# One slot for a batch's value matmuls, maxima split on GpSimd, and another order of the prologue, in a fused attention and feed-forward block

## What is computed

```python
x = x + tanh(g_xattn) * xattn(layernorm(x), ctx, ctx)     # per head: q, k, v are 8 x 256
    # qk = einsum('dq,dl->ql', q, k) / sqrt(8); sm = softmax(qk); out = einsum('ql,dl->dq', sm, v)
x = x + tanh(g_ffn) * ffn(layernorm(x))
    # a = quant8(x) @ ternary(w_gate).T ; b = quant8(x) @ ternary(w_up).T      (256 -> 1024)
    # h = silu(a) * b ; h = rms_norm(h, ln_weight) ; quant8(h) @ ternary(w_down).T (1024 -> 256)
```

## Time and profile before

| | us |
|---|---|
| median of 3 runs | 220.3 |
| lowest, highest | 218.5, 220.82 |
| the profiled execution | 220.69 |
| its span, first to last instruction | 218.9 |

### The profile page before, as it was taken

One profiled execution on the slowest core, in us unless ns is written; L12 is line 12 of the kernel. 1 busy time (PEld: TensorE's weight loads), 2 busy tenths in 40 slices (PEclk: granted clock), 3 DMA queues, 4 the chain that ended last, 5 costly groups with the idle time before them and its releaser, 6 DMA issues. The chain is left out here.

```text
span 218.9 us, 3965 instructions
## 1 busy us (share of the span) xinstructions
PE 155.9 (71%) x1307; PEld 79.6 (36%) x1314; DVE 168.5 (77%) x343; ACT 133.4 (61%) x265; POOL 110.4 (50%) x195
## 2 busy tenths in 40 slices
PE   0023886839895898979898998999988972463343
PEld 0021442424452534434355553645533441230221
DVE  6818999725775767489896988889849979899981
ACT  3400426816899896948678586869879872163330
POOL 5824868835600598598838875758741103111010
PEclk9999999976999999999999999999999999589555
DMA  3496799899692644272163156121021100000001
GB/s 96 133 206 183 217 352 369 227 307 314 158 270 53 160 130 125 57 214 78 31 171 93 40 132 163 30 76 32 27 76 34 46 28 0 9 15 24 0 0 48
DMA packets 21955, 25.85 MB, mean 118 GB/s; under 512 B 4374, under 2 KB 18966, under 8 KB 20918
## 3 DMA queue, kind: packets, MB, share of 16 engines
q1 hardware_dynamic: 20040, 21.36, 35.2%
q10 hardware_dynamic: 1896, 4.26, 5.9%
HBM read 18.20 MB, written 7.19 MB: 116 GB/s over the span
## 5 line engine op out<-in xcount | busy, mean ns | idle before, releaser
L935 DVE TENSOR_REDUCE mx<-sr 128x2 f32<-128x512 f32 x128 | 82.1, 679 | 16.9 <-PE sr L1212 16.6
L718 ACT ACTIVATE pr<-sr 128x512 f32<-128x512 f32 x128 | 71.4, 601 | 13.3 <-PE sr L1234 12.9
L1212 PE MATMUL sr<-ks,qs 128*128 128x256 bf16 x256 | 51.5, 298 | 24.0 <-DMA ks<-scr_k 19.4
L1234 PE MATMUL sr<-qs,ks 128*128 128x256 bf16 x256 | 49.1, 278 | 5.8 <-DVE kh L1022 2.9
L1247 PE MATMUL ob<-pr,vw 128*32 128x256 f32 x512 | 41.1, 394 | 3.5 <-ACT pr L718 2.1
L1212 PEld LDWEIGHTS sr<-ks,qs 128*128 128x128 bf16 x256 | 21.3, 104 | 52.7 <-issue 25.1
L1234 PEld LDWEIGHTS sr<-qs,ks 128*128 128x128 bf16 x256 | 22.1, 99 | 18.0 <-DVE kh L1022 3.8
L1287 PE MATMUL sr<-wt,xt 128*128 128x512 bf16 x57 | 16.1, 407 | 3.2 <-ACT xt L758 2.0
L1321 PE MATMUL sr<-wt,ht 128*128 128x256 bf16 x64 | 10.7, 316 | 9.0 <-ACT ht L816 5.3
L1247 PEld LDWEIGHTS ob<-pr,vw 128*32 128x32 f32 x512 | 10.3, 108 | 18.0 <-ACT pr L718 9.7
L768 ACT ACTIVATE kh<-sr,ghs 128x512 f32<-128x512 f32 x16 | 10.9, 687 | 7.6 <-PE sr L1287 7.5
(11 more groups left out here) (123 smaller groups left out, 249.9 us busy)
## 6 DMA issues: line engine op xcount, KB each, us to landing
qs<-scr_q SPq DMA_DIRECT2D x7, 576.0 KB
ks<-scr_k SPq DMA_DIRECT2D x21, 192.0 KB
scr_o<-osb SPq DMA_DIRECT2D x14, 128.0 KB, 3.8
scr_k<-kp SPq DMA_DIRECT2D x8, 192.0 KB, 5.3
scr_q<-qp SPq DMA_DIRECT2D x8, 192.0 KB, 5.4
scr_k<-kp SPq DMA_DIRECT2D x8, 128.0 KB, 5.5
wf<-in_wg ACTq DMA_DIRECT2D x1, 1024.0 KB, 7.1
wf<-in_wu ACTq DMA_DIRECT2D x1, 1024.0 KB, 10.3
```

Source lines behind the costliest of these rows:

```text
L718: nc.scalar.activation(pr[:, b % PR_BUFS, m % 4, :], bank("score", m)[:, :], ACT.Exp, scale=float(DH) ** -0.5).then_inc(exp_done, 1)
L935: nc.vector.tensor_reduce(mx[:, h % 2, first + 2 * at:first + 2 * at + 2], bank("max", n)[:, :].rearrange("p (c n) -> p c n", c=KC), axis= ...
L1212: mm = nc.tensor.matmul(bank("max", n)[:, c * COLS:(c + 1) * COLS], qs[:, t % STACKS, at:at + P], ks[:, t % STACKS, u * COLS:(u + 1) * COL ...
L1234: mm = nc.tensor.matmul(bank("score", m)[:, c * COLS:(c + 1) * COLS], ks[:, t % STACKS, at:at + P], qs[:, t % STACKS, u * COLS:(u + 1) * C ...
```

## The change

- A batch's value matmuls, c = 0 and c = 1, run in one slot, VALUES = 6 after the batch's first score.
- POOL splits a group's maxima in slot hi into a bf16 part and the remainder (split_maxima). PE transposes both with one bf16 transposition in slot hi + 4, ACT casts them into the rows that SP writes in hi + 5. cut_maxima, its padding and constants go away.
- Prologue: pair 0 of x and context and the three gates are loaded right after tiles 0 and 1; the mean of pair 0 comes before the second and third memset of qs. split_pair becomes five parts with slots of their own; so do first_parts and second_parts on ACT.
- LATE, LATE_NORM = 6, 7: tiles 4 and 5 are weighed and scaled on POOL, tiles 5 and 6 get attention and norm there. Slots in AT and the other tables are changed. The weights are loaded in slots 5, 18, 24.

```diff
--- before.py
+++ after.py
@@ -28,16 +28,15 @@
 VBUFS = 3
 
 LAG = 20
+VALUES = 6
 PR_BUFS = 3
-LATE, LATE_NORM = 4, 5
+LATE, LATE_NORM = 6, 7
 BANKS = 7
 TURNED = TILES - 1
-CAST = 3
-CUT = 3
-SHIFT = 4
-TURN = 3
-PAD = 16
-SMALL = PAD + 2 * 8 + PAD + 2 * 4
+CAST = 4
+SPLIT = 0
+SHIFT = 5
+TURN = 4
...
-    "copy1": [37, 55, 72, 86, 104, 119, 133, 150],
-    "invert": [48, 64, 79, 94, 112, 124, 138, None],
-    "inv_out": [44, 61, 82, 95, 108, 124, 140, None],
-    "inv_in": [47, 61, 82, 98, 118, 124, 147, None],
-    "attention": [53, 68, 83, 97, 115, 128, 149, 155],
-    "norm": [58, 73, 90, 104, 124, 133, 150, 166],
-    "scale_x": [62, 76, 92, 110, 124, None, None, None],
-    "weigh": [80, 86, 106, 117, None, None, None, None],
-    "scale_y": [80, 94, 110, 127, 140, 165, 176, 189],
-    "down": [97, 109, 128, 139, 156, 172, 187, 199],
-    "result": [98, 110, 127, 137, 164, 168, 194, 208],
+    "copy1": [38, 55, 70, 85, 102, 118, 133, 151],
+    "invert": [54, 60, 78, 95, 110, 126, 138, None],
+    "inv_out": [48, 61, 82, 94, 106, 126, 150, None],
+    "inv_in": [53, 62, 82, 94, 113, 128, 151, None],
+    "attention": [58, 69, 86, 101, 114, 131, 146, 157],
+    "norm": [65, 73, 92, 105, 123, 131, 149, 166],
+    "scale_x": [68, 75, 93, 111, 123, 138, 154, None],
+    "weigh": [84, 89, 107, 118, 139, 153, None, None],
+    "scale_y": [86, 97, 112, 127, 139, 165, 176, 192],
+    "down": [101, 111, 130, 138, 157, 185, 199, 211],
+    "result": [101, 111, 129, 136, 165, 181, 207, 231],
...
-PAIR_AT = [0, 18, 30]
-LOAD_AT = [0, 2, 10]
-VALUES_AT = 16
-WEIGHT_AT = [12, 27, 33]
-ABS_AT = [43, 48, 51]
-ROUND_AT = [53, 57, 69]
-CUT_AT = [57, 58, 71]
-NORM_W_AT = 65
+MEAN_AT = [17, 18]
+NORM_AT = [0, 18, 26]
+CUT_K_AT = [0, 17, 40]
+CUT_Q_AT = [0, 21, 36]
+LAST_K_AT = [1, 32, 47]
+LAST_Q_AT = [2, 35, 51]
+FIRST_K_AT = [0, 16, 31]
+FIRST_Q_AT = [0, 25, 33]
+NEXT_K_AT = [6, 19, 44]
+NEXT_Q_AT = [1, 31, 36]
+PARTS_AT = [1, 30, 42]
+LOAD_AT = [0, 2, 5]
+GATES_AT = 0
+VALUES_AT = 19
+WEIGHT_AT = [5, 18, 24]
+ABS_AT = [46, 49, 50]
+ROUND_AT = [54, 58, 68]
+CUT_AT = [52, 61, 77]
+NORM_W_AT = 64
 SUM_W_AT = 52
-STACK_AT = 4
-FILL_AT = [4, 13, 20]
-CONST_AT = 31
+STACK_AT = [23, 41, 48, 66, 84, 97]
+FILL_AT = [7, 16, 21]
+CONST_AT = 3
...
-        mx = sb("mx", [P, 2, SMALL + 2 * 4 + 2 * 4], F32)
-        mh = sb("mh", [2 * 2 * 8, 2, P], BF16)
+        mx = sb("mx", [P, 2, 2 * 8], F32)
+        mxp = sb("mxp", [P, 2, 2, 2 * 8], BF16)
...
@@ -390,6 +399,9 @@
 
             load_xk(0, 1, 0)
             load_xk(1, 2, 1)
+            load_pair(0)
+            for n, g in enumerate((gx_d, gf_d, gamma_d)):
+                sp.dma_start(gates[:, n:n + 1], g.rearrange("(a n) -> a n", a=1).to_broadcast((P, 1))).then_inc(gate_in, DMA)
             sp.wait_ge(k2_cast, 1)
             sp.wait_ge(k3_done, 1)
             k_to_dram(0)
@@ -399,7 +411,6 @@
             sp.wait_ge(k_out[0], 2 * DMA)
             sp.wait_ge(k_ones, 1)
             load_keys(0, 0, HALF, early_in)
-            load_pair(0)
             sp.wait_ge(k2_cast, 2)
             sp.wait_ge(k3_done, 2)
             k_to_dram(1)
@@ -407,8 +418,6 @@
             sp.wait_ge(q3_done, 2)
             q_to_dram(1)
             load_keys(0, HALF, SPAN, stack_in[0])
-            for n, g in enumerate((gx_d, gf_d, gamma_d)):
-                sp.dma_start(gates[:, n:n + 1], g.rearrange("(a n) -> a n", a=1).to_broadcast((P, 1))).then_inc(gate_in, DMA)
             next_stack(1)
             load_values(0, 0, 2)
 
@@ -418,12 +427,12 @@
                 for pair in range(PAIRS):
                     if pair >= 1 and n == LOAD_AT[pair]:
                         load_pair(pair)
-                    if n == PAIR_AT[pair] + 12:
+                    if n == PARTS_AT[pair]:
                         parts_to_dram(pair)
                 if n == VALUES_AT:
                     load_values(1, 2, TILES)
-                if n % PER == STACK_AT and 2 <= n // PER + 1 < TILES:
-                    next_stack(n // PER + 1)
+                if n in STACK_AT:
+                    next_stack(2 + STACK_AT.index(n))
                 for r in range(2):
                     t = due(f"sums{r}", n)
                     if t is not None and t < TURNED:
...
+            def norm_pair(pair):
 
                 two = slice(2 + 2 * pair, 4 + 2 * pair)
-                q = qf[:, two, :].rearrange("p t n -> p (t n)")
-                k = kh[:, two, :].rearrange("p t n -> p (t n)")
                 rstd_q(two.start, two.stop)
                 step(nc.gpsimd.tensor_scalar(nm[:, two], mv[:, two, 0], -1.0, None, ALU.mult))
                 pool.wait_ge(q_rstd, two.stop)
                 for t in range(two.start, two.stop):
                     nc.gpsimd.tensor_scalar(qf[:, t, :], xh[:, t, :], nm[:, t:t + 1], rs[:, t:t + 1],
                                             ALU.add, ALU.mult).then_inc(q_normed, 1)
+
+            def cut_keys(pair):
+
+                k = pair_of(kh, pair)
                 pool.wait_ge(k1_cast, 3 + pair)
                 nc.gpsimd.tensor_tensor(k, k, high_half(k), ALU.subtract).then_inc(k1_left, 1)
+
+            def cut_queries(pair):
+
+                q = pair_of(qf, pair)
                 pool.wait_ge(q1_cast, 3 + pair)
-                pool.wait_ge(q_normed, two.stop)
+                pool.wait_ge(q_normed, 4 + 2 * pair)
                 nc.gpsimd.tensor_tensor(q, q, high_half(q), ALU.subtract).then_inc(q1_left, 1)
+
...
+            def split_maxima(h):
+
+                rows = group_rows(h)
+                pool.wait_ge(max_taken, GROUPS[h][1])
+                if h >= 2:
+                    pool.wait_ge(max_turned, h - 1)
+                parts = mxp[:, h % 2, :, :].rearrange("p n r -> p (n r)")
+                high = high_half(mx[:, h % 2, :])[:, 0:rows]
+                nc.gpsimd.tensor_copy(parts[:, 0:rows], high).then_inc(max_split, 1)
+                nc.gpsimd.tensor_tensor(parts[:, rows:2 * rows], mx[:, h % 2, 0:rows], high, ALU.subtract).then_inc(max_split, 1)
 
...
+                if n - SPLIT in ENDS:
+                    split_maxima(ENDS[n - SPLIT])
                 if n in FILL_AT:
                     first_values(FILL_AT.index(n))
-                for pair in range(1, PAIRS):
-                    if n == PAIR_AT[pair]:
-                        split_pair(pair)
+                for pair in range(PAIRS):
+                    if n == NORM_AT[pair]:
+                        norm_pair(pair)
+                    if n == CUT_K_AT[pair]:
+                        cut_keys(pair)
+                    if n == CUT_Q_AT[pair]:
+                        cut_queries(pair)
+                    if n == LAST_K_AT[pair]:
+                        last_keys(pair)
+                    if n == LAST_Q_AT[pair]:
+                        last_queries(pair)
                 if n == CONST_AT:
                     late_constants()
                 if p == 0 and VBUFS <= T < TILES:
-                    pool.wait_ge(pv_done, 8 * (T - VBUFS + 1))
+                    pool.wait_ge(pv_done, 4 * (T - VBUFS + 1))
                     fill_values(T)
...
                                      scale=float(DH) ** -0.5).then_inc(exp_done, 1)
@@ -723,12 +752,12 @@
                 rows = 2 * group_rows(h)
                 act.wait_ge(max_turned, h + 1)
                 if h >= 2:
-                    act.wait_ge(max_cut, h - 1)
-                nc.scalar.activation(mh[0:rows, h % 2, :], bank("turn", h)[0:rows, 0:P], ACT.Copy).then_inc(max_cast, 1)
+                    act.wait_ge(shift_in[h % 2], shifts_in(h - 2))
+                nc.scalar.activation(mp[0:rows, h % 2, :], halves_of("turn", h)[0:rows, 0, :], ACT.Copy).then_inc(max_cast, 1)
...
                 if 0 <= n - LAG < TOTAL:
                     exp(n - LAG)
                 for pair in range(PAIRS):
-                    if n == PAIR_AT[pair] + 4:
-                        first_parts(pair)
-                    if n == PAIR_AT[pair] + 8:
-                        second_parts(pair)
+                    if n == FIRST_K_AT[pair]:
+                        act.wait_ge(k_in[2 + pair], DMA)
+                        key_pair(pair, 0, k1_cast)
+                    if n == FIRST_Q_AT[pair]:
+                        act.wait_ge(q_normed, 4 + 2 * pair)
+                        query_pair(pair, 0, q1_cast)
+                    if n == NEXT_K_AT[pair]:
+                        act.wait_ge(k1_left, 3 + pair)
+                        key_pair(pair, 1, k2_cast)
+                    if n == NEXT_Q_AT[pair]:
+                        act.wait_ge(q1_left, 3 + pair)
+                        query_pair(pair, 1, q2_cast)
+                if n == GATES_AT:
+                    act.wait_ge(gate_in, 3 * DMA)
+                    nc.scalar.activation(tg[:, :], gates[:, 0:2], ACT.Tanh).then_inc(tanhed, 1)
                 if n in WEIGHT_AT:
...
+            def mean_pair(pair):
+                dve.wait_ge(x_in[2 + pair], DMA)
+                for t in (2 + 2 * pair, 3 + 2 * pair):
```

(50 more changed lines are left out.)

100 lines of the change are left out of this document (40 added, 60 removed), and 18 rows, old and new, of the table AT.

## The result

| | before | after |
|---|---|---|
| median, us | 219.87 | 223.36 |
| lowest to highest | 218.5 to 220.82 | 222.37 to 224.1 |
| span of the profiled execution | 218.9 | 220.9 |
| mean granted clock | 0.933 | 0.883 |

The changed kernel is slower: ratio 1.0136, 95% interval 1.0084 to 1.0189, where 206 us was forecast. The stretch from maximum 64 to 127 and the tail became a little shorter; the loss stands before maximum 32, where the largest single gain was expected.

What follows compares the result with a forecast made beforehand. PE was taken to set the pace in slots 64 to 128, DMA share 0.90 the early stretch, DVE the tail. Gains of 5 + 2.5 + 3 + 1 + 3 = 14.5 us gave a 204.4 span, said as 206 us; range 199 to 216.

Steps and rivals of the forecast that it cites:

- The prologue's first maximum: Prologue: first maximum starts at 15.4 instead of 20.27 us, 4.9 earlier, with PE's first matmul at 14.8.
- The weights are also loaded earlier … I take 5 us by maximum 32: Up to maximum 32: 5 us gained despite earlier weight loads in a stretch of DMA share 0.90; bounds 2 and 8.
- The prediction's own sign of being wrong: Wrong if the first maximum starts early but maximum 32 does not, or POOL's splits start over four slots late.
- rival (2): Early stretch: DMA eats the early gain, stack 2 lands near 47 as before; 9.5 gained, 211 us; chance 0.10.
- The split behind the first fill: Early stretch: POOL's first fill, waiting for a values load, precedes group 1's split; could eat some of the 5 us.
- Rival (4): Slots 56 to 144: split behind late POOL work, PE waits at each transposition; slower, 227 us; chance 0.08.
- Values in one slot: Value matmuls: sixteen records together in 1.00 us save PE 0.25 a batch, 32 batches; bounds 0.11 and 0.36.
- The transposition: Transposing maxima: one bf16 transposition for a float32 one saves PE 0.60 us a group, 18 groups.
- Slots 64 to 128: Middle: PE paces and gives back 8.8 us, POOL's load grows to 62; stretch 71, 3 us gained; bounds 0 and 8.8.
- Slots 32 to 64: PE gives back 4.4 of 34.8 us, 1.9 off for SP's waiting writes and shift; 2.5 gained; bounds 0 and 5.
- 128 to the last value matmul: Slots 128 to 148: ACT busy 19.23 of 22.1 us, its work unchanged; 1 us gained; bounds 0 and 2.
- Tail: After the last value matmul: DVE sheds 5.6 of 31.76 us, POOL's chain grows; 3 us gained; bounds -2 and 6.

Runs made afterwards that it cites:

- e5: Kernel before with only the prologue's new order (pair 0, gates, mean of pair 0), weights at old slots: 217.75 us, ratio 0.9892 to before.
- e4: Kernel before with only a batch's value matmuls put in one slot: 220.16 us, ratio 1.0001 to before.
- e20: Kernel before with only the two more tiles on GpSimd and the new AT slots for tiles 4 to 7: 220.31 us, ratio 1.0073 to before.
- e16: e5 with the weights loaded at slots 5, 18, 24 instead of 12, 27, 33: 222.4 us, ratio 1.0096 to before.
- e11: Changed kernel with the weights loaded at the old slots 12, 27, 33: 219.03 us, ratio 1.0027 to before.
- e1: Changed kernel with POOL's first fill of values in slot 9 instead of 7: 222.71 us, ratio 1.0096 to before.
- e2: Changed kernel with the split of maxima on DVE instead of POOL, same slot: 220.33 us, ratio 0.9947 to before.
- e13: e9 with transposition 3 and shift 4 slots after the group, split on POOL: 243.63 us, ratio 1.115 to before.
- e12: e10 with transposition 3 and shift 4 slots after the group, split on DVE: 217.0 us, ratio 0.9939 to before.
- e19: e12 with the two more tiles on GpSimd and the new AT slots for tiles 4 to 7: 217.25 us, ratio 0.9795 to before.
- e3: Changed kernel with e1 and e2 together (later first fill, split on DVE): 218.62 us, ratio 0.9894 to before.
- e14: Changed kernel with e11, e1 and e2 together (old weight slots, later fill, split on DVE): 218.51 us, ratio 1.001 to before.
- e9: Changed kernel's forms with all slots of the kernel before, tiles 4 to 6 in DVE's form, split on POOL: 238.04 us, ratio 1.0769 to before.
- e10: e9 with the split of maxima on DVE instead of POOL: 230.23 us, ratio 1.0428 to before.
- e7: Changed kernel with tiles 4 to 6 back in DVE's form: 225.09 us, ratio 1.0208 to before.

## Why the prediction was wrong

**The prologue's first maximum** was right in kind and mis-sized: 16.94 instead of 15.4. I held PE's first matmul at 14.8; it went to 16.3. The first write went out at 5.23, 0.1 later, so the five issues cost nothing on SP, as said; but the loads of pair 0 and the gates are now issued ahead of that write, and SP, which waits for the write to land, issues the first keys at 9.40, for 7.68 before. The term of 4.9 measured 3.3, and in e5 2.8; against the 19.2 to 19.4 that two executions with the old prologue show (e4, e20) it is about 2.

**"The weights are also loaded earlier … I take 5 us by maximum 32"** is the step that failed: 5 us of gain forecast, 4.1 of loss measured. It named the DMA share of 0.90 and the moved loads, and then priced them at nothing. In this stretch a load moved ahead of a stack delays it: 1 MB is 3.8 us by rate and 4.65 as measured in e16, and with the weights back at their slots maximum 32 of the changed kernel comes 5.1 earlier (e11). The prediction's own sign of being wrong came true: the first maximum is early and maximum 32 is not. My bounds of 2 and 8 held no loss at all, though rival (2) had said that the early gain could be eaten; it took "stack 2 lands near 47 as before" as the worst, and stack 2 let PE go on at 51.60. The issue slots in the diff were enough to price it.

**The split behind the first fill** was seen too ("now stands ahead of the split of group 1. Of these any can eat some") and priced at nothing for the same 5 us. The wait was 9.24. Alone it is worth little (e1: 0.65), since the keys stand 4.98 behind it; with the rest on DVE it is 3.0 (e2).

**Rival (4)** had 0.08 and the wrong place. That its 227 us is the nearest figure to 223.4 is luck. Its mechanism is real and up to 26.6 us big (e13), but in the changed kernel PE's waits for the split between maxima 64 and 127 come to 1.6 us (the three longest of PE there; then DVE's longest):

```profile
PE sr L1298 <- ACT xi L780: 3.2, 1, 3.2
PE sr L1257 <- DVE mx L972: 2.1, 1, 2.1
PE sr L1247 <- POOL mxp L573: 1.6, 2, 0.9
```

```profile
DVE am L1005 <- POOL xn L592: 7.4, 4, 3.1
```

The waits for xn and xi, 3.7 and 0.8 us in the kernel before, look like work that is late because it stands behind the split on POOL. The split is not their main cause: with it on DVE at the same slots (e2), PE waits 3.4 us for xi there and DVE 5.0 for xn. Which of the other new slots makes them longer was not measured. The groups of after, busy and mean ns as in the earlier trace rows, with the idle time before:

```profile
L572 POOL COPY mxp<-mx 128x16 bf16<-128x16 bf16 (+1 forms) x18 | 3.5, 195 | 14.1 <-DVE mx L972 14.1
L573 POOL TENSOR_TENSOR mxp<-mx 128x16 bf16<-128x16 f32 (+1 forms) x18 | 3.8, 212 | 0.0
L625 POOL TENSOR_TENSOR wf<-wf,lnw 128x1024 f32<-128x1024 f32 x6 | 14.2, 2360 | 2.4 <-DVE wf L1059 2.4
```

The split itself costs 0.41 a group against 0.5 forecast. The copy of 16 columns took 197 ns and that of 8 columns 190, so nearly all of it does not depend on the width.

**Values in one slot**: right in size by starts, 16 records in 1.00 (112.08 to 113.08; by busy time e4 gives back 2.8 of the 4.0 counted from maximum 64 on), and wrong in what it is worth: e4 gives nothing.

**The transposition** saves 0.40, not 0.60: its record takes 0.16 and 0.09 stand ahead of it. After, at 109.6 (compare):

```profile
109.27 0.38 PE L1237 MATMUL sr<-ks,qs 128*128 128x256 bf16 x2
109.58 0.23 PE L1247 MATMUL sr<-identb,mxp 128*32 128x128 bf16 x1
109.74 0.39 PE L1257 MATMUL sr<-qs,ks 128*128 128x256 bf16 x2
```

The change of form costs a bf16 transposition of 32 columns too, which I had left out. In e12, with before's slots, values and transposition together can't be told from e5 without them (217.0 for 217.75, ratios 0.994 and 0.989).

**Slots 64 to 128**: 3 us forecast, 1.4 measured, POOL busy 58.94 where I had 62. "PE sets the pace" was read from a busy share of 67.7 in 74.2. In 15 kernels of this study PE is busy between 61.6 (e12, e19) and 67.7 (before, e20) and the stretch takes 72.8 to 75.9, which follows it weakly (a straight line through the 15 gives 0.18 us for each us of PE); e3 and e14 do less in it, e9, e10 and e13 wait for the split or the shift. The clearest pair is e5 and e12, both at full clock: PE is busy 6.0 us less in e12 and the stretch is 0.7 shorter. So PE's busy time alone does not set it. What does was not isolated: DVE's 59.1 to 63.9 don't order it either, and what is left are the waits of the engines for each other. (The cut ends at the start of the last maximum, so the 74.2 us hold 63 slots of 1.18 and not 64 of 1.16; no term changes by it.)

**Slots 32 to 64**: the SP step was right, PE waits 2.5 for a shift and 1.9 for keys. Instead of 2.5 gained it is 0.7 lost. **128 to the last value matmul**: 1 forecast, 0.6 lost: the two more tiles put POOL's 16.54 us there (5.21 before). **Tail**: 3 forecast, 2.0 measured, right within its bounds; DVE is busy 25.91 for 31.76.

**The account.** By medians: prologue −2.8 (e5), weights +4.65 (e16), split on GpSimd +3.0 (e2), two tiles from −1.7 (e7) to +0.5 (e20), values and transposition 0 to −0.75 (e12 against e5): together from +2.4 to +5.4, measured +3.5. By the ratios the same terms come to +2.1 to +4.1%, for 1.4% measured, so the agreement of the medians is no proof: the terms overlap (e14), and the effect of the other new slots was not measured apart. What is shown is the sign and size of the weights' term, twice (e16 and e11).

## What to carry to other kernels

In a stretch whose DMA share is 0.9, price every load that the diff moves ahead of another by its bytes over the stretch's rate, and subtract it from the gain before anything else; here the load stood on ACT's queue and the stack's loads on SP's. When two short instructions move to another engine, their cost is what stands in front of them in that queue, and a slot's worth of slack on one queue (the shift on SP) has to be checked against what the tables issue in the same slots. Time that a busy engine gives back is a gain only if removing work from it alone, in a run, moves the stretch.

## What the runs showed of the hardware that was not expected

- The half clock showed little cost where loads set the pace and much where PE had work waiting. To maximum 32 the changed kernel has a granted clock of 0.78 (partly at 1.2 GHz instead of 2.4) and e16 one of 0.97, and maximum 32 comes at 52.3 and 51.7; the two kernels differ in more than the clock, so this is not isolated. In e13's middle each of five waits of PE of 1.9 to 4.8 us has a stretch at 1.2 GHz right behind it (96.1 to 102.9 us, at 0.50, behind the wait of 4.75 that ends at 96.75); the mean is 0.87, and PE is busy 9.3 us longer than in e12.
- A switch from score matmuls to a bf16 transposition of 32 columns and back costs 0.09 us beside the record's 0.16 (109.27 to 109.74), near the 0.11 that float32 values cost in the earlier trace rows.
- Two instructions of 0.20 and 0.21 us on GpSimd, moved from VectorE, made one kernel 26.6 us slower and another 12.2.
